# Start-up order, joined kernel sum and last products of a two-layer adapter network

## The reference

```
w = L0_cond_weight[itok_B_3_7]                 # one 512x512 matrix per item, adapters 3 to 7
h = einsum('bsi,boi->bso', x, w)
x = x + h @ kernel + bias + (per-group LoRA of h, rank 32) + (shared LoRA of h, rank 32)
g, u = x W_gate' , x W_up'  (each + LoRA of adapter itok_B_2_6, rank 16)
down = silu(g) * u @ W_down' (+ LoRA)          # inner size 1376
scores = down @ gate_w' + gate_b ; the best of four ranks (8, 16, 32, 64) is chosen
x = x + down @ W' + b + (A, B cut to the chosen rank)
```

## Time and profile before

| | |
|---|---|
| median of 3 runs | 700.91 us (700.26 to 701.99) |
| the profiled execution's own time | 702.66 us |
| its span, first to last instruction | 700.6 us |
| PE busy | 675.9 us, 96% |
| DVE, ACT, POOL busy | 313.4, 296.5, 340.0 us |
| mean granted TensorE clock | 0.996 |

### The profile page before, as it was taken

The page is one execution under the profiler, slowest core; times in us unless marked ns, Lnnn a source line. Parts: engine busy times, 40 slices in busy tenths (PEclk is TensorE's granted clock), DMA queues, the critical chain, the costliest instruction groups (busy, mean ns, idle before and its releaser), DMA issues. The chain is left out here.

```text
span 700.6 us, 11139 instructions
## 1 busy us (share of the span) xinstructions
PE 675.9 (96%) x3353; PEld 561.6 (80%) x3353; DVE 313.4 (45%) x739; ACT 296.5 (42%) x642; POOL 340.0 (49%) x262
## 2 busy tenths in 40 slices
PE   4799989999999999999999999999999999999997
PEld 3578778887788888888888888888888888887775
DVE  3788567746521223731222562142373124234664
ACT  2776543334643343653333464343365343344210
POOL 0034400141787666487766578776648867400000
PEclk9999999999999999999999999999999999999999
DMA  8973561031354336254335245433424524200112
GB/s 322 349 265 136 196 225 61 15 98 47 109 165 145 111 114 240 79 168 155 111 109 172 63 142 167 138 112 120 155 80 154 166 85 137 85 0 1 61 67 113
DMA packets 32210, 91.80 MB, mean 131 GB/s; under 512 B 5312, under 2 KB 5440, under 8 KB 30624
## 3 DMA queue, kind: packets, MB, share of 16 engines
q1 hardware_dynamic: 21936, 61.05, 25.9%
q0 software_dynamic: 10080, 30.16, 12.9%
q10 hardware_dynamic: 144, 0.00, 0.0%
HBM read 81.23 MB, written 9.96 MB: 130 GB/s over the span
## 5 line engine op out<-in xcount | busy, mean ns | idle before, releaser
L570 POOL TENSOR_TENSOR gu_lo<-gu_raw,gu_hi 128x1024 fp32r<-128x1024 f32 x44 | 113.7, 2584 | 101.2 <-ACT gu_hi L646 100.2
L1263 DVE TENSOR_TENSOR act_f<-psU,silu 128x512 f32<-128x512 f32 x44 | 30.4, 692 | 187.7 <-ACT silu L819 95.8
L601 POOL DMA_INDIRECT ab<-in_ab,idx_tab x88 | 86.6, 984 | 20.7 <-issue 16.2
L819 ACT ACTIVATE silu<-psG 128x512 f32<-128x512 f32 x44 | 26.2, 597 | 153.0 <-issue 89.1
L1380 PE MATMUL psD<-act_hi,dn_hi 128*128 128x512 f32 x176 | 69.0, 392 | 0.0
L1381 PE MATMUL psD<-act_lo,dn_hi 128*128 128x512 f32 x176 | 69.0, 392 | 0.0
L1382 PE MATMUL psD<-act_hi,dn_lo 128*128 128x512 f32 x176 | 68.6, 390 | 0.0
L570 POOL TENSOR_TENSOR dn_lo<-dn_raw,dn_hi 128x512 fp32r<-128x512 f32 x44 | 57.3, 1303 | 21.0 <-ACT dn_hi L646 20.9
L575 POOL DMA_INDIRECT h_scratch<-h,idx_s x22 | 23.7, 1077 | 64.1 <-ACT h L675 32.7
L1380 PE MATMUL psG<-x_hi,gu_hi 128*128 128x512 f32 x132 | 54.2, 411 | 0.6 <-ACT silu L819 0.6
L1382 PE MATMUL psG<-x_hi,gu_lo 128*128 128x512 f32 x132 | 51.7, 392 | 0.0
(11 more groups left out here) (346 smaller groups left out, 1706.4 us busy)
## 6 DMA issues: line engine op xcount, KB each, us to landing
gu_raw<-in_gu SPq DMA_DIRECT2D x44, 512.0 KB
dn_raw<-in_dn SPq DMA_DIRECT2D x44, 256.0 KB
cond_w_raw<-in_cond_w SPq DMA_DIRECT2D x8, 1024.0 KB, 7.3
x_all<-in_x_t SPq DMA_DIRECT2D x4, 1024.0 KB, 10.7
tok<-h_scratch SPq DMA_DIRECT2D x4, 1024.0 KB, 5.5
out_t<-x_all SPq DMA_DIRECT2D x16, 256.0 KB, 2.1
ab<-in_ab,idx_tab POOLq DMA_INDIRECT x88
kraw<-in_kern SPq DMA_DIRECT2D x1, 1024.0 KB, 12.2
```

The source lines that it names most:

```text
L570: pool.tensor_tensor(dst, x, hi, ALU.subtract).then_inc(s, 1)
L601: pool.indirect_dma_start(ab[:, par, g, :], None, a["ab"], bass.IndirectOffsetOnAxis(idx_tab[:, NGT * t + g, fc:fc + 1], 0)).then_inc(S[f" ...
L819: act.activation(silu[:], psG[:], ACT.Silu).then_inc(S["silu_s"], 1)
L1263: dve.tensor_tensor(act_f[:], psU[:], silu[:], ALU.mult).then_inc(S["act_f_s"], 1)
```

## The change

- The constants come in two parts from ACT's queue: 64 rows of what the sort needs, then the rest. DVE no longer takes the shared LoRA's rest before the one-hot.
- SP loads three copies of the shared LoRA on three groups of 32 partitions, so that one K = 96 product holds all three terms: 4 products in place of 12.
- SP loads x in two halves with the first weight between them. The second half waits until POOL has issued two gathers (`xg_sent`); the weights 1 and 2 wait until all of x is there.
- The token rows of blocks 0, 1 and 2 are gathered from x by POOL with an index from the sort, turned by PE (`turn_x`), rounded by ACT straight out of PSUM. Three products of the identity (`warm`) stand before block 0.
- The results of blocks 4 to 7 go to four further places (`h0_far`), so that there are eight before one is used again.
- Within the blocks, weight k is rounded in the odd block 2k-1, behind the items of that block; before, it stood in the even block 2k-4, between two blocks' items. The kernel sum is made in four parts in blocks 10, 12, 14 and 15; `lora_a` is loaded after that, `lora_b` after block 18.
- After the blocks the kernel's rounding is done in four parts, and the second half of `gsel` times `lora_b` stands behind `turn_h0(0)`.
- At the end `turn_scores` comes before `linear(0)` for all but the first tile; in the last tile the mask is turned after `linear(1)`, and three LoRA products stand in the middle of `linear(3)`.

```diff
@@ SP
-            sp.dma_start(const[:, 0:CONST_EARLY], a["const"][:, 0:CONST_EARLY]).then_inc(S["const_in"], 16)
-            sp.dma_start(sh[:], a["shared"]).then_inc(S["shared_in"], 16)
-            for t in range(NTB):
+            for k in range(3):
+                sp.dma_start(sh[k * RANK0:k * RANK0 + RANK0], a["shared"]).then_inc(S["shared_in"], 16)
...
+            load_x(0)
+            load_x(1)
...
             sp.wait_ge(S["order_ready"], 1)
-            for k in range(3):
-                load_w(k)
-            sp.dma_start(kraw[:], a["kern"]).then_inc(S["kraw_in"], 16)
-            sp.dma_start(gate_v[:], a["gate"]).then_inc(S["gate_in"], 16)
-
+            load_w(0)
+            sp.wait_ge(S["xg_sent"], 1)
+            load_x(2)
+            load_x(3)
+            sp.wait_ge(S["x_all_in"], 16 * NTB)
+            load_w(1)
+            load_w(2)
@@ POOL
+            pool.wait_ge(S["idx_x_ready"], 1)
+            for b in range(AHEAD):
+                pool.indirect_dma_start(h0[:, b, :], None, a["x"], bass.IndirectOffsetOnAxis(idx_x[:, b:b + 1], 0)
+                                        ).then_inc(S[f"xg_in{b}"], 16)
+                if b == 1:
+                    pool.tensor_copy(sent[:], idx_x[:]).then_inc(S["xg_sent"], 1)
@@ ACT
+            act.wait_ge(S["w_in0"], 16)
+            high_w0(0)
+            high_xg(0)
+            for c in range(1, C):
+                high_w0(c)
+            folded(2)
+            high_xg(1)
+            folded(3)
+            high_xg(2)
             act.wait_ge(S["item_ready"], 1)
...
                 if b + AHEAD < NBLK:
                     high_xs(b + AHEAD)
-                if b % W_EVERY == 0 and b // W_EVERY + 2 < N_COND:
-                    high_w(b // W_EVERY + 2)
+                if b in SPLIT_AT:
+                    high_w(SPLIT_AT[b])
@@ DVE
-            dve.wait_ge(S["sh_hi_s"], 1)
-            low(sh_lo[:], sh[:], sh_hi[:], S["sh_lo_s"])
             dve.wait_ge(S["const_in"], 16)
...
+            scatter_rows()
+            low_w0(0)
+            low_xg(0)
+            for c in range(1, C):
+                low_w0(c)
+            low_xg(1)
+            low_xg(2)
@@ PE
+            def turn_x(b):
+                pe.wait_ge(S[f"xg_in{b}"], 16)
+                if b == 2:
+                    pe.wait_ge(S["idx_ready"], 1)
+                for c in range(C):
+                    mm = pe.transpose(X_BANK[b][:, c * P:c * P + P], h0[:, b, c * P:c * P + P], ident)
+                mm.then_inc(S["xg_ps"], 1)
...
+                    if b == 0 and c == 1:
+                        turn_x(1)
...
+            turn_x(0)
+            warm(psG[:, 0:P], 3)
...
+            two_blocks_b(0)
             pe.wait_ge(S["aeff_done"], 2)
...
             turn_h0(0)
+            two_blocks_b(1)
...
-                for o in range(C):
+                if t:
+                    turn_scores()
+                    linear(0)
...
+                    turn_mask()
+                    linear(2)
+                    linear(3, range(2))
+                    lora(0)
+                    lora(1)
+                    lora(2)
+                    linear(3, range(2, C))
+                lora(3)
```

More of the change, by code:

```diff
@@ L84 @@
 CONST_N = _at
+CONST_SORT = CONST_AT["ident"]
 CONST_EARLY = CONST_AT["group_mask"]
@@ L455, in split_w @@
             return C + e
+        KERN_AT = {10: 0, 12: 1, 14: 2, 15: 3}
+        SPLIT_AT = {2 * k - 1: k for k in range(1, N_COND)}
         def evacuated(eng, b):
@@ L1464, in _ @@
                 cond(b, e)
+                if b == 0:
+                    turn_x(2)
                 e = after
@@ L1478, in _, with two_blocks_b @@
             pe.wait_ge(S["lb_lo_s"], 1)
-            for j in range(NTB // 2):
+            def two_blocks_b(j):
                 for k in range(4):
@@ L1672, in second_layer, with linear @@
                 hi, lo = HT2[t % 2]
-                def linear(o):
+                def linear(o, part=range(C)):
                     if t:
                         pe.wait_ge(S["out_v"], C * (t - 1) + o + 1)
-                    for c in range(C):
+                    for c in part:
                         mm = product(psD[:, o, :], both(wf_hi, wf_lo, al, c, slice(o * P, o * P + P)),
@@ L1680, in linear @@
                     return mm
-                linear(0)
-                pe.wait_ge(S["r_sb"], 2 * t + 1)
-                for s in range(SUB):
-                    mm = pe.transpose(psG[:, s * NR:(s + 1) * NR], scores[RMAX:RS, s * P:(s + 1) * P],
-                                      ident[RMAX:RS, RMAX:RS])
-                mm.then_inc(S["sc_ps"], 1)
-                linear(1)
-                linear(2)
-                pe.wait_ge(S["mexp_s"], NR * (t + 1))
-                pe.wait_ge(S["xa_m"], 2 * t)
@@ L1692, in second_layer, with turn_scores @@
[L1692 to L1699 removed]
+                def turn_scores():
+                    pe.wait_ge(S["r_sb"], 2 * t + 1)
+                    for s in range(SUB):
+                        mm = pe.transpose(psG[:, s * NR:(s + 1) * NR], scores[RMAX:RS, s * P:(s + 1) * P],
+                                          ident[RMAX:RS, RMAX:RS])
+                    mm.then_inc(S["sc_ps"], 1)
@@ L1700, in second_layer, with turn_mask, lora @@
+                def turn_mask():
+                    pe.wait_ge(S["mexp_s"], NR * (t + 1))
+                    pe.wait_ge(S["xa_m"], 2 * t)
+                    for s in range(SUB):
+                        pe.transpose(psU[0:RMAX, s * P:(s + 1) * P], mexp[:, s, :], ident).then_inc(S["mask_ps"], 1)
+                def lora(o):
+                    if o == 0:
+                        pe.wait_ge(S["xa_hi"], t + 1)
+                        pe.wait_ge(S["xa_lo"], t + 1)
                     stacked(psD[:, o, :], rb[:, o * P:o * P + P], r64_hi[:], r64_lo[:], False, True
```

255 lines of the change are left out of this document (155 added, 100 removed).

## The result

The changed kernel takes 694.66 us (median of 4 runs, 693.49 to 694.8), the kernel before 701.4 beside it: ratio 0.9896, interval 0.9879 to 0.9912, 6.7 us less. In a second batch the same pair stood at 693.29 and 701.24, ratio 0.9889 (0.9873 to 0.9904), 8.0 us less. The profiled execution after took 694.61 us with a span of 692.7, against 702.66 and 700.6 before; the profiled execution before was 1.3 us above the median of its kernel, the one after was not.

A forecast was written before the change was run, and what follows sets the result against it. PE, busy 96% of the span, was taken as the bound, so only its waits, low clock and the ends could be won. Start 2.5, after the blocks 3.2, end 1.0 sum to 6.7 us: median 694.2, range 691.6 to 697.6.

The forecast's parts named there:

- the landing of the first weight goes by the bytes ahead of it: Start: fewer bytes queued ahead, one and a half gathers included, land the first weight 3.7 us earlier, at 17.0.
- Block 0: Start: its first product comes at 19.4, 3.1 us earlier: weight landing plus 1.84 and 0.6 us.
- Warm products: Start: the three products ahead of block 0 stand in PE's wait for ACT and DVE and cost nothing.
- The second weight: Start: it lands at 29.3, is rounded by 33.5 and wanted at block 5 at 35.9: slack 2.4 us.
- nothing to win: Blocks 1 to 21: PE is busy 58.10 of 58.15 us, so no gain there.
- After the blocks: First transpose to first kernel product: gain 3.2 us if PE keeps the upper clock, 1.6 if not.
- the token tile: After the blocks: its landing at 95.7 is what is late next and leaves PE a wait of 0.7 us.
- The end: Last tile: earlier softmax chain and DVE additions under later products gain 1.0 us, between 0.3 and 1.2.
- The start gives nothing: Rival: gathers land after the weight, or the second weight overruns its slack; 696.7 us, chance 0.16.
- slower: Rival: weights chained behind all of x come late, decisive if x lands from 32.0 on; chance 0.03.
- The lower clock stays: Rival: low clock remains after the blocks and in block 0, losing 1.6 and 0.7 us; 696.5 us, chance 0.14.
- The clock is up with block 0: Rival: PE, fed from 16 on, has the upper clock at block 0, 1.3 us more; 692.9 us, chance 0.12.

The follow-up runs named there:

- before again: The kernel before, unchanged, profiled once more: one run, 700.06 us.
- weight first: The changed kernel with the first weight issued ahead of the second quarter of x: 695.14 us, ratio 0.9916.
- the end put back: The changed kernel with the last layer's order of before in all four tiles: 694.5 us, ratio 0.9909.
- Middle put back: The changed kernel with all lora_b products and the kernel's rounding ahead of the transposes again: 694.72 us, ratio 0.9924.
- half: The changed kernel with six of the second group's twelve gsel times lora_b products ahead of the token transposes instead of behind: 691.95 us, ratio 0.9874.
- half, own weight: The changed kernel with six lora_b products ahead of the transposes and blocks 16 and 17 waiting for their own weight alone: 691.43 us, ratio 0.9861.

## Why the prediction was right, and where it was not

**Forecast and total.** 694.2 forecast, 694.66 measured, 6.7 us saved as summed. That it is so near is in part luck. The second batch has 8.0 for the same pair, and profile against profile it is 8.0 too, 694.6 for the forecast 696.0. Between these two profiles the start and what follows it up to the `gsel` products brought 4.5 us for the 2.5 of the sum, the middle 2.3 for 3.2, the rest 1.15 for 1.0. The profile before began late, though. An estimate for its usual execution is "before again" with the 1.2 us of the lower clock added, 699.2 us of span where the three batches have medians of 699.2 to 699.6: then it is 3.1, 2.3 and 1.1 us. Either way one error is up and one down.

**The first weight: the rule held, two terms of it didn't.** The step "the landing of the first weight goes by the bytes ahead of it" gave 17.0. It landed at 14.9, and at 13.7 to 14.0 in most later profiles. From issue to landing the loads of x in front took (the four of the kernel before, issued at 2.5 to 4.5; the first two of the changed one, issued at 2.9 and 3.6):

```profile
DMA to landing us min/median/max: 7.9/10.7/13.7
```

```profile
DMA to landing us min/median/max: 6.7/7.6/8.6
```

So they landed from 10.3 to 18.2 and the weight at 20.7 before, and at 9.6 and 12.1 and the weight at 14.9 now: one behind another, 2.4 to 2.8 us for each MB, as 420 GB/s would have it. What failed is 0.9 us for one and a half gathers ahead of the weight (the first landed at 15.5, behind it) and 1.1 us in front: the first load of x landed 0.8 us earlier than before, although 145 KB more (0.35 us) are ahead of it. Three variants took 1 MB from ahead of the weight, and it came 0.3 us earlier, not 2.4. In "weight first" the one load ahead of it landed at 8.7 and the weight was issued at 8.8, with nothing ahead of it; it took 4.9 us, near the 5.4 for 1 MB from an empty queue. A second bound stands close behind the bytes: the issue, and with it the sort (`w_order` at 7.73, issue at 8.90). The order was wrong as well: in this profile the gathered copy, forecast at 16 ahead of the weight and there at 15.6, is what block 0 waits for, and in the executions with an earlier start PE's own one-hot products end just then too (14.4). Behind it come 2.75 us of transposing and rounding, most of which the sum had laid under the wait for the weight.

**Block 0.** Forecast 19.4, measured 18.32 (17.2 to 17.5 in most, 19.7 at the latest): the weight 2.1 us earlier, and 3.4 us from it to block 0 for the 2.4 of the sum, since the copy came last. Block 0 to block 1 was forecast at 5.4 and took 5.43: the two transposes at 1.3 less 0.7 from the clock came out right as a sum. Warm products cost nothing, right: block 0 begins at 17.40 without them too. They bring 0.7 to 1.2 us through the clock, where the prediction had 0.7 for them and the transposes together.

**The second weight.** All of x was forecast at 22.9 and the weight's rest at 33.5; SP issues the next weights at 24.1 and DVE's rest ends at 33.3. With block 5 wanted at 34.8 the slack was 1.5 for the forecast 2.4. The items of block 5, which DVE takes behind the rest, leave less: they end at 34.1, and in the execution of the end put back the product that waits for them starts at 34.5, 0.3 before block 5 is wanted here. In that execution it was wanted 0.9 before it could start. It takes both an early start and a late x: there SP issued the weight at 24.2. "Middle put back", "half" and "half, own weight" began as early, issued it at 22.5 to 23.0 and lost nothing at block 5. A start earlier by another us would meet this bound.

**The blocks: "nothing to win" was wrong both ways.** PE busy 58.10 of 58.15 us hides waits, because a product's record lasts 0.39 us and its distance to the next is 0.23. In the kernel before, eight of the 20 distances from block to block behind block 1 are 2.77 to 2.91 us, the others 2.72. The unit price of 0.231 has this in it; undisturbed it is 0.227. Such a place, from PE's timeline of the kernel before, in front of block 4 (0.41 us between starts for 0.23, and a weight's rest of 2.29 us ahead of the items on DVE):

```profile
35.25 0.39 PE L1457 MATMUL psD<-cond_w_lo,xs_t_hi 128*128 x1
35.66 0.49 PE L1455 MATMUL psD<-cond_w_hi,xs_t_hi 128*128 x1
```

With the items ahead of the weights these 1.0 us are gone, and I had not looked for them. They pay for what I had not seen either, from the timeline of the changed kernel:

```profile
62.80 2.29 DVE L940 TENSOR_TENSOR cond_w_lo<-cond_w_raw,cond_w_hi 128x2048 fp32r<-128x2048 f32 x1 [0.59 <-ACT cond_w_hi L691]
...
65.00 0.48 DVE L940 TENSOR_TENSOR xs_t_lo<-x_all,xs_t_hi 128x128 fp32r<-128x128 f32 x2
65.23 0.49 PE L1550 MATMUL psD<-cond_w_hi,xs_t_hi 128*128 x1 [0.32 <-DVE cond_w_lo L940]
```

From block 16 on, `cond` waits for the rests of all weights, weight 7's among them, which block 18 is the first to use and which is now taken in block 13 instead of block 10. I had checked when each weight is wanted by its own block and not which count the wait names. The net of the blocks is 0.2.

**After the blocks: 3.2 forecast, 2.3 in the profile.** From the first transpose to the first kernel product it was 7.5 us and is 6.4 with twelve products of 2.8 us in between: 3.8 us won for the 3.9 of the sum. The eight products took 3.50 us and take 1.85, the 1.6 that the sum gave to the lower clock; by "before again" 1.2 of it are the clock's and 0.4 the wider distances right behind the splitting (2.28 us at 1.00). The term that failed is the token tile, forecast to keep PE 0.7 us. It kept it 1.5: the wait before the `gsel` products shrank by 0.7, so that PE was ready 4.3 us behind the tile's issue and not 4.75, and the landing took 5.7 us for 5.4. What PE gains ahead of the token tile is lost in front of it, until other work stands there. The step "what is late next is the token tile" was right, and it named the remedy that the six products are.

The 1.6 for the lower clock was read from one profile, and "before again", without such a stretch, leaves only 1.1 for the whole step. By the granted clocks of the 29 runs the first profile is the usual case, so the term stands for the median. But it doesn't belong to this edit alone: with the new start and the old middle the clock stayed up in five of six runs, after the same wait of 2.1 us, and with the old start and the new middle the profile shows no stretch either. By these runs either part of the change takes the lower clock away in most executions; what decides it is open.

**The end.** Forecast 1.0, measured 1.07 (0.48 up to the last product and 0.59 behind it, for 0.35 and 0.65), and 1.05 with the end put back.

**The rivals.** "The start gives nothing" and "slower": not so; x landed by 24, far from 32. "The lower clock stays": the granted clock is 1.00 from the transposes to the kernel products, behind a wait of 1.5 us and transposes of 1.75, and none of the nine runs of the changed kernel is below a mean of 0.999. That is also against what the prediction took the rule of the Trainium skill's page on transposes to give. "The clock is up with block 0": in none of the ten profiles with the warm products at its first product; the distances fell from 0.43 to 0.23 us between 0.9 and 3.6 us behind it.

## What to carry to other kernels

A wait that a matmul's record can cover (here up to 0.16 us at a time) shows in no busy share: lay the distances between the first products of equal blocks side by side and look at those that are longer. For a transfer whose issue hangs on computed values, work out both its issue with the time to land from an empty queue (here 13.7) and the bytes ahead of it (14.0): the later one counts, and moving bytes wins no more than the difference. Before a term of the sum rests on a clock level seen in one profile, look at the mean granted clock of all runs; a second profile alone would have misled here. And when the bound after an edit is a landing, put work in front of it rather than behind.

## What was not expected of the hardware

- A scatter's issue on POOL, 0.97 us alone, took 2.42 us where a weight's rest of 2.29 us on DVE had begun before it, and up to 4.99 when DVE ran four operations with two SBUF inputs back to back; in a neighbouring profile, with 0.1 us between two of them, the same scatter took 1.37. The 22 scatters took 23.7 us of POOL before and 33.1 after the change, because it puts ACT's copies, and so the scatters, beside DVE's rests. Two of the eleven profiles with the new blocks show a 4.99.

```profile
L575 POOL DMA_INDIRECT h_scratch<-h,idx_s x22 | 23.7, 1077 | 64.1 <-ACT h L675 32.7 <-DVE h L1082 28.7 <-issue 2.7
```

```profile
L614 POOL DMA_INDIRECT h_scratch<-h,idx_s x18 | 26.3, 1462 | 33.4 <-ACT h L723 18.8 <-DVE h L1156 14.2 <-issue 0.3
L614 POOL DMA_INDIRECT h_scratch<-h_far,idx_s x4 | 6.8, 1692 | 3.0 <-DVE h_far L1156 1.7 <-ACT h_far L723 1.3
```

  These are the groups of POOL's scatters by line (count, busy us, mean ns, idle before and releasers), of the kernel before and of the changed one.
- A gather of 256 KB takes 3.8 and 4.1 us from issue to landing (medians of three, two profiles) where the loads in front of it are held back, 4.9 to 6.0 where they are not. The first one, issued at 10.1 to 10.3 in all, was there at 14.7 in one execution and at 17.0 in another of the same load order, together with the weight issued before it.
- The same wait of 2.1 us in the same code was followed by a granted clock of 0.50 in one execution and of 1.00 in another; by the mean clocks of 29 runs the first is the rule.
